# Graph attention on one core: a unit's normalising multiply on ScalarE instead of VectorE, its reciprocal earlier on VectorE

## What is computed

```python
h = maximum(layernorm(x), 0)
hW = (h @ W.T).reshape(n, 8, 32)
attn = s_src[:, None, :] + s_dst[None, :, :] + adj[:, :, None] * We[:, 0] + be
attn = leaky_relu(where(adj > 0, attn, -inf), 0.2)
attn = softmax(attn, axis=1)
out = x + einsum('ijh,jhd->ihd', attn, hW) + h @ Wr.T + br
```

## Time and profile before

| | us |
|---|---|
| median of three runs | 2366.17 |
| lowest, highest | 2361.86, 2367.48 |
| profiled execution, own time | 2366.95 |
| its span | 2365.2 |
| VectorE busy in it | 2042.5 (86%) |
| POOL busy in it | 1607.2 (68%) |
| ScalarE busy in it | 1080.1 (46%) |
| PE busy in it | 1011.7 (43%) |

### The profile page before, as it was taken

One profiled execution on the slowest core, in us unless ns is written; L12 is line 12 of the kernel. 1 busy time (PEld: TensorE's weight loads), 2 busy tenths in 40 slices (PEclk: granted clock), 3 DMA queues, 4 the chain that ended last, 5 costly groups with the idle time before them and its releaser, 6 DMA issues. The chain is left out here.

```text
span 2365.2 us, 22833 instructions
## 1 busy us (share of the span) xinstructions
PE 1011.7 (43%) x3773; PEld 798.4 (34%) x3774; DVE 2042.5 (86%) x5463; ACT 1080.1 (46%) x4646; POOL 1607.2 (68%) x1939
## 2 busy tenths in 40 slices
PE   4766304422453274336333543362344336353344
PEld 3555203322432153325322433252234225242232
DVE  4899798899699679998988899999999998888733
ACT  2333206532574264446544645453453446475454
POOL 5444476667676677667777777677677775677775
PEclk9988656666765566666666766676666666677676
DMA  6444876677676867787777688788888886777443
GB/s 145 158 144 139 298 211 167 196 232 229 138 210 216 233 165 223 233 247 213 238 230 227 190 254 254 236 244 255 254 259 245 258 263 189 207 215 207 99 89 67
DMA packets 167080, 489.46 MB, mean 207 GB/s; under 512 B 35888, under 2 KB 54360, under 8 KB 166728
## 3 DMA queue, kind: packets, MB, share of 16 engines
q1 hardware_dynamic: 86088, 278.11, 36.0%
q0 software_dynamic: 80848, 209.94, 34.5%
HBM read 451.08 MB, written 36.83 MB: 206 GB/s over the span
## 5 line engine op out<-in xcount | busy, mean ns | idle before, releaser
L600 POOL DMA_INDIRECT arena<-table,arena x1262 | 1285.7, 1019 | 504.3 <-issue 316.3
L1304 PE MATMUL banks<-arena,ident 128*128 128x264 f32 x1566 | 501.8, 493 | 1206.3 <-DVE arena L904 1206.3
L1304 PEld LDWEIGHTS banks<-arena,ident 128*128 128x128 f32 x1566 | 386.2, 252 | 1319.0 <-issue 1092.4
L1172 ACT ACTIVATE arena<-arena 128x32 f32<-128x32 f32 x3832 | 819.3, 306 | 2.2
L746 DVE FIND_INDEX8 work<-work,adj_sb 128x8 uint32<-128x502 f32 (+56 forms) x775 | 667.0, 865 | 0.0
L757 DVE MAX8 work<-adj_sb 128x8 f32<-128x502 f32 (+56 forms) x775 | 652.1, 856 | 0.0
L1166 ACT ACTIVATE arena<-pre 128x104 f32<-128x104 f32 (+22 forms) x81 | 23.2, 302 | 998.2 <-DVE pre L894 998.2
L1310 PE MATMUL banks<-arena,ident 128*128 128x264 f32 x958 | 253.8, 407 | 39.2 <-ACT arena L1172 38.8
L904 DVE TENSOR_TENSOR arena<-arena 128x1024 f32<-128x1024 f32 (+8 forms) x169 | 226.3, 1388 | 37.4 <-ACT arena L1166 37.3
L1310 PEld LDWEIGHTS banks<-arena,ident 128*128 128x128 f32 x958 | 181.7, 196 | 99.4 <-ACT arena L1172 71.9
L1156 ACT ACTIVATE pre<-arena,we_all 128x13 f32<-128x13 f32 (+26 forms) x536 | 165.2, 406 | 87.7 <-DMA arena<-lists 87.7
(11 more groups left out here) (127 smaller groups left out, 931.8 us busy)
## 6 DMA issues: line engine op xcount, KB each, us to landing
adj_sb<-in_adj_dram SPq DMA_DIRECT2D x505, 512.0 KB, 4.6
arena<-table,arena POOLq DMA_INDIRECT x1262, 4.0
table<-arena POOLq DMA_DIRECT2D x32, 264.0 KB, 2.6
arena<-in_x_dram SPq DMA_DIRECT2D x32, 256.0 KB, 2.9
resid<-arena POOLq DMA_DIRECT2D x32, 256.0 KB, 2.6
out_dram<-arena POOLq DMA_DIRECT2D x32, 256.0 KB, 2.8
adj_sb<-in_adj_dram SPq DMA_DIRECT2D x1, 1536.0 KB, 23.1
lists<-arena,rank POOLq DMA_INDIRECT x67, 3.8
```

The costliest lines, as they stand in the source:

```text
L600: pool.indirect_dma_start(gath[:, un.slot(k), :], None, table[:, :], bass.IndirectOffsetOnAxis(ap=rec[:, k, 0:1], axis=0)).then_inc(lane, 16)
L1172: last = s.activation(g, g, ACT.Copy, scale=gath[:, un.slot(k), HD + h:HD + h + 1])
L1304: last = m.matmul(ps_sum[:, u % 2, :], ident[:, :], gath[:, un.slot(k), :], start=(k == 0), stop=False)
```

## The change

`evacuate` is split. VectorE keeps the wait for the sums, the copy of the partial units and the reciprocal (`invert`), and does them for the unit before at m = 4, behind the last score step of the present unit and ahead of `weight`. ScalarE does the multiply (`evacuate`), in eight instructions of 32 columns with the head's reciprocal as scale, behind the exponential of the present unit and ahead of its weighting. The wait for the output buffer (the store of six units before) goes with it. The last unit is evacuated on ScalarE behind the loop.

```diff
-            def evacuate(un):
+            def invert(un):
 
                 u = un.u
                 dve.wait_ge(S["tile_sum"], u + 1)
                 if un.partial:
                     v.tensor_copy(ml[:, u, H:ML], ps_sum[:, u % 2, HD:ROW])
                 v.reciprocal(rinv[:, u % 2, :], ps_sum[:, u % 2, HD:ROW]).then_inc(S["recip"], 1)
-                if u >= OUTS:
-                    landed(dve, units[u - OUTS].store_seq + (2 if units[u - OUTS].partial else 1))
-                dve.wait_ge(S["recip"], u + 1)
-                v.tensor_tensor(out_sb[u % OUTS].rearrange("p (h d) -> p h d", d=D),
-                                ps_sum[:, u % 2, 0:HD].rearrange("p (h d) -> p h d", d=D),
-                                rinv[:, u % 2, :].unsqueeze(2).to_broadcast([P, H, D]), ALU.mult).then_inc(S["evac"], 1)
...
                     softmax_step(un, m)
+                    if m == 4 and un.u:
+                        invert(units[un.u - 1])
                 weight(un)
...
-                if un.u:
-                    evacuate(units[un.u - 1])
...
-            evacuate(units[-1])
+            invert(units[-1])
...
                 last.then_inc(S["exped"], 1)
+                if u:
+                    evacuate(units[u - 1])
                 act.wait_ge(S["exped"], u + 1)
...
+            def evacuate(un):
+
+                u = un.u
+                act.wait_ge(S["recip"], u + 1)
+                if u >= OUTS:
+                    landed(act, units[u - OUTS].store_seq + (2 if units[u - OUTS].partial else 1))
+                for h in range(H):
+                    last = s.activation(out_sb[u % OUTS][:, h * D:(h + 1) * D], ps_sum[:, u % 2, h * D:(h + 1) * D],
+                                        ACT.Copy, scale=rinv[:, u % 2, h:h + 1])
+                last.then_inc(S["evac"], 1)
...
+            evacuate(units[-1])
```

## The result

| | before | after |
|---|---|---|
| median of six runs, us | 2365.73 | 2352.35 |
| lowest, highest | 2361.86, 2367.48 | 2349.73, 2357.16 |
| profiled execution, own time | 2366.95 | 2354.80 |
| its span | 2365.2 | 2353.0 |
| VectorE busy | 2042.5 | 2013.1 |

The ratio is 0.9949, with a 95% interval of 0.9936 to 0.9962: the changed kernel is faster by 13.4 us (9 to 15), where 12.0 were forecast. Lines have moved: the ring's sums are L1312 and L1318 now, the exponential L1160, the weighting on ScalarE L1168, the new multiply L1178.

A forecast was written before the change was run, and what follows sets the result against it. VectorE was taken to set the pace from 1523 to 1994 us, POOL elsewhere; 10.8 us there plus 1.2 at the release make 12.0 off 2366.95; less 0.78 for the median, 2354.2 us, range 2349 to 2360.5.

The forecast's parts named there:

- Where VectorE sets the pace: From 1523 to 1994 us VectorE was taken to set the pace, so its savings count only there.
- A unit's saving: VectorE in units 26 to 44: 0.68 us removed, 0.08 put back, 0.60 saved; 18 units give 10.8 us.
- Rival A: The reciprocal at m = 4 still holds VectorE 0.34 us, so a unit saves 0.34; 2359.6 us, chance 0.12.
- The block on ScalarE: Eight multiplies per unit behind the exponential were to take 1.9 us, at most 3.8.
- The release 1.2 us earlier: Unit 44's evacuation, which frees POOL's store, was to be ready at 1992.7 instead of 1993.94 us.
- POOL's remaining wait of 7.7 us: At unit 44's store POOL was still to wait 7.7 us, so VectorE would still decide.
- The cap of 19.4 us: Largest gain before POOL never waits at the stores of units 43 and 44: 19.4 us.
- rival D: Removing the pair opens further waits the rows don't name, so the gain reaches POOL's cap; 2346.8 us, chance 0.05.
- The tail at 0: From unit 46 on, ScalarE's longer chain was to fit POOL's room; 0, with 0 to 1.5 us of loss.
- rival C: In tail units without a find, the chain ScalarE, PE, reciprocal, `weight` closes and delays POOL; 2375 us, chance 0.05.
- Rival B: Later gathers or adjacency pieces make units 27 to 30 wait, giving back some 6 us; 2360 us, chance 0.08.
- The end at 0: Unit 66 and the closing flag loops: ScalarE's delay mostly lies under PE; 0, from -0.3 to +1.5 us.

The follow-up runs named there:

- the change inside only: The change applied to the evacuations of units 26 to 44 alone, all others left on VectorE as in the kernel before; 2351.98 us, ratio 0.9946.
- before with the moved slots: Kernel before, with ScalarE instead of VectorE weighting two more slots per unit in units 27 to 44; 2361.13 us, ratio 0.9962.
- after again: The changed kernel, unaltered, measured once more beside the slot runs on the same chip; 2357.53 us, ratio 0.9944 to the kernel before.
- the change outside only: The change applied to units 0 to 25 and 45 to 66, the old evacuation kept for 26 to 44; 2373.51 us, ratio 1.0016.
- the clean slots: Changed kernel, ScalarE weighting two more slots per unit in units 27 to 44 except 28, 36 and 44; 2351.14 us, ratio 0.9939.

## Why the prediction was right

The time was forecast at 2354.2 us and came at 2352.35, for the main reason given; two steps behind it were wrong and did not show in the sum. Step by step:

- **Where VectorE sets the pace: held.** Units 26 to 44 alone give all the gain, the others none (no loss to 8 us of loss).
- **A unit's saving: 0.60 us forecast (0.34 to 0.68), 0.66 measured**, 11.8 instead of 10.8 us in all. The step that was slightly mis-sized is the reciprocal at m = 4: it was booked at 0.08 us and cost nothing in unit 45, since L799 already waited 0.37 us there. Rival A (0.34 us each) is excluded by the 453.2 us; the reciprocal run alone shows how the sum splits, 0.33 and 0.33.
- **The block on ScalarE: 1.9 us forecast, 1.53 measured.** The weighting L1168 starts 0.21 us apart in sequence ((8.60 - 0.34) / 39), the new multiply 0.18 us apart ((1.53 - 0.30) / 7), 36 ns less. The Trainium skill gives ScalarE a fixed cost of 224 cycles with a source in SBUF and 172 in PSUM, at 1.2 GHz (VectorE: DVE Perf Modes, "The TRN2 errata — SBUF-src ops pay a fixed extra latency per instruction"); its figures make that an estimated 43 ns less, near what the rows show. The Trainium skill's advice in the same section against many small tiles did not become a cost, because the eight small ones ran on an engine that was idle. (L1132 was not the only row with a source in PSUM, as the prediction has it: L1122 takes 576 ns for 512 columns, 32 times. The sum does not use it.)
- **The release 1.2 us earlier: right in itself, worth nothing in the profile.** From L883 of unit 45 the evacuation is ready after 3.75 us (1982.10 - 1978.35), before after 5.46 (1993.94 - 1988.48): 1.7 us earlier. But POOL was not there yet; the piece went from 5.74 to 5.79 us.
- **POOL's remaining wait of 7.7 us: wrong.** It was 0 in both profiles of after, 2.06 us in the kernel with the change inside only. The step took POOL's own pace from one profile and held it fixed. From the end of unit 27's last gather to POOL's arrival at the store of unit 44, POOL took 457.8 us in the profile of before, its wait of 5.9 us taken out, and 465.4 in that of after: 7.6 us more. Unit 27's last gather ended another 2.0 us later (1518.47 against 1516.46). The two make up the 9.6 us by which POOL came later than forecast. The change need not be the cause: before with the moved slots has 465.4 too, the reciprocal alone 462.1, and before's own is the shortest of the twelve profiles with the stores in this place. In this pair POOL's waits for landings of its gathers between 1523 and 1970 us went from 25.7 to 32.9 us, and those for landings of stores from 4.3 to 10.2; the second profile of after has 26.3 and 8.9 with a pace of 464.2, so they do not settle it either. The rows of after:

```profile
POOL arena L600 <- DMA arena<-table,arena: 32.9, 52, 2.0
POOL arena L600 <- DMA out_dram<-w_all,arena: 10.2, 8, 2.0
```

- **The cap of 19.4 us (rival D): too high for the same reason.** With 8 us more off VectorE the gain is 14.4 us (17.6 by the medians, 19.2 at the interval's end), while POOL waits for neither VectorE nor ScalarE at the stores of units 43 and 44.
- **The tail at 0 (0 to 1.5 loss): held**, at -0.8. The waits of find-less units for their sums grew as rival C has it, from 4.2 us (once) to 37.8, and POOL passed none of them on ahead of the last gather:

```profile
DVE rinv L913 <- PE banks L1318: 37.8, 8, 6.0
...
1991.34 0.21 DVE L913 RECIPROCAL rinv<-banks 128x8 f32<-128x8 f32 x1 [5.90 <-PE banks L1318]
```

  Unit 61's ranking was the right place to watch; the doubled block reached it and cost some 8 us there.
- **Rival B: not seen.** Within the stretch no wait for gathers came up. The start is 1.7 us later in the profiled pair and L883 waits 8.64 us for its gathers, not 3.82; but of the 4.8 us more, 3.1 are VectorE's coming earlier (1516.55 against 1519.67). And 1.7 us mean nothing here: before with the moved slots has the same instructions as before up to this row, and after again the same as after, and their starts are 5 us off, one to each side:

```profile
1518.19 0.42 DVE L883 TENSOR_TENSOR pre<-pre,arena 128x128 f32<-128x128 f32 x2
...
1530.56 0.44 DVE L883 TENSOR_TENSOR pre<-pre,arena 128x128 f32<-128x128 f32 x2 [9.09 <-DMA arena<-table,arena]
```

- **The end at 0 (-0.3 to +1.5): -1.3.** The last unit's block runs beside the flags' rows and the last store waits 4.0 us for it, behind POOL's last gather, where it is not the end that it holds up:

```profile
2336.70 0.21 DVE L913 RECIPROCAL rinv<-banks 128x8 f32<-128x8 f32 x1 [4.36 <-PE banks L1318]
2336.95 1.53 ACT L1178 ACTIVATE w_all<-banks,rinv 128x32 f32<-128x32 f32 x8 [1.40 <-DVE rinv L913]
2338.75 1.56 POOL L616 DMA_INDIRECT out_dram<-w_all,arena  x1 [3.97 <-ACT w_all L1178]
```

So 1.0 us more in the stretch and 2.1 in tail and end stand against 1.2 lost at the release and 1.7 at the start: the total of 12.15 in the profiled pair is as close to 12.0 as it is partly because these cancel, which is luck: the start alone differs by more between executions of one kernel.

## What to carry to other kernels

Cut the kernel into stretches by who sets the pace, and count an instruction's saving only in those where its engine does: here 18 of 67 units paid, and a row's gap between two dependent instructions told that a short one could be placed there for nothing. Work handed to an idle engine is free only until a chain through it closes; look for the consumer with the least room (unit 61's ranking, 0.8 us), where POOL waited 9 to 11 us once the work was doubled. And do not take the second engine's wait in one profile as a reserve: once it stops waiting, its own pace, which differed by 12 us between profiles here, is the next limit.

## What the runs showed of the hardware

- A ScalarE multiply of 128x32 with a pointer as scale starts every 0.18 us from PSUM (eight in 1.53 us), every 0.21 us from SBUF (40 in 8.60 us).
- The time in which POOL issues the gathers of units 28 to 48 (from the end of unit 27's last to unit 48's last, waits for an evacuation taken out) was 457.8 us before, 459.7 with the change outside only, 462.1 with the reciprocal alone, 465.4 in before with the moved slots; 465.4 and 464.2 in two profiles of after, 461.5 with the clean slots, 459.7 with the block doubled everywhere and 469.6 with the early block doubled. POOL's instructions are the same. What makes it slower or faster is not settled by these runs.
